# A gated MLP with LoRA, then a LoRA output layer, on one core: three small reorderings of who does what when

## The reference, cut to what matters

```python
x = x.reshape(8, 256, 1024)                       # f32, 2048 tokens of 1024 features
# layer 0: gate, up and down, each with a LoRA pair chosen by batch (rank 16)
gate = x @ W_gate.T + 0.5 * (x @ A_gate[i0[b]].T) @ B_gate[i0[b]].T       # 2752 features
up   = x @ W_up.T   + 0.5 * (x @ A_up[i0[b]].T) @ B_up[i0[b]].T
act  = silu(gate) * up
x = x + act @ W_down.T + 0.5 * (act @ A_down[i0[b]].T) @ B_down[i0[b]].T
# layer 1: output layer with its own adapters
x = x + x @ weight.T + bias + scale[i1[b]] * (x @ a_out[i1[b]].T) @ b_out[i1[b]].T
```

## Time and profile before

| | us |
|---|---|
| median of three runs (1677.37 to 1678.23) | 1678.08 |
| the profiled execution's own time | 1679.92 |
| its span, first to last instruction | 1678.2 |
| PE busy | 1625.1 (97%) |
| DVE busy | 1130.0 (67%) |
| POOL busy | 661.6 (39%) |
| ACT busy | 501.7 (30%) |
| mean granted TensorE clock | 0.990 |

### The profile page before, as it was taken

The page is one execution under the profiler, slowest core; times in us unless marked ns, Lnnn a source line. Parts: engine busy times, 40 slices in busy tenths (PEclk is TensorE's granted clock), DMA queues, the critical chain, the costliest instruction groups (busy, mean ns, idle before and its releaser), DMA issues.

```text
span 1678.2 us, 20940 instructions
## 1 busy us (share of the span) xinstructions
PE 1625.1 (97%) x7060; PEld 1318.2 (79%) x7060; DVE 1130.0 (67%) x1298; ACT 501.7 (30%) x833; POOL 661.6 (39%) x445
## 2 busy tenths in 40 slices
PE   5799999999998999999999999999999999899998
PEld 4588888888876888888888778888888887678886
DVE  4977777777768777777776655666665577766343
ACT  3543333333345433333334221111111122331100
POOL 4255444444452544454444443333332331541110
PEclk9899999999999999999999999999999999999999
DMA  8344434423532334344334751122222220113322
GB/s 151 81 104 105 141 92 108 150 79 84 136 89 78 102 104 142 93 115 141 82 89 129 246 146 60 48 79 79 79 57 73 69 63 13 26 31 78 79 46 56
DMA packets 218126, 156.13 MB, mean 93 GB/s; under 512 B 110692, under 2 KB 200164, under 8 KB 215268
## 3 DMA queue, kind: packets, MB, share of 16 engines
q1 hardware_dynamic: 170048, 115.18, 27.2%
q10 hardware_dynamic: 47844, 39.59, 7.4%
q0 software_dynamic: 128, 0.00, 0.0%
HBM read 115.38 MB, written 39.32 MB: 92 GB/s over the span
## 4 chain that ended last, share of the span: by engine, by line
PE 65%; DVE 1%; DMA 1%; SPq 1%; issue 0%; ACT 0%; DVEq 0%
PE ps L1892 65%; DMA Ad_raw<-in_L_cond_A_down_dram 1%; SPq L1261 0%; DVE acc L915 0%; SPq L1243 0%; DVE turned L850 0%; DVE Bd L861 0%; DVE Ad_turned L874 0%; DVE xt L593 0%; DVE ct L1033 0%; DVE turned L845 0%; DVE Td L933 0%; DVE c21buf L675 0%; DVE co L1055 0%; ACT W L1349 0%
## 5 line engine op out<-in xcount | busy, mean ns | idle before, releaser
L1892 PE MATMUL ps<-act,Wd 128*128 128x512 f32 x2016 | 463.7, 390 | 2.7 <-DVE acc L915 1.6
L1892 PE MATMUL ps<-X_T,W 128*128 128x512 f32 x1944 | 461.9, 393 | 0.4 <-DVE X_T L597 0.3
L1892 PEld LDWEIGHTS ps<-act,Wd 128*128 128x128 f32 x2016 | 379.2, 188 | 84.0 <-DVE acc L915 2.5
L1892 PE MATMUL ps<-X_B,W 128*128 128x512 f32 x1728 | 420.1, 393 | 20.1 <-DVE X_B L597 17.4
L1892 PEld LDWEIGHTS ps<-X_T,W 128*128 128x128 f32 x1944 | 366.0, 189 | 83.9 <-DVE vbuf L662 5.2
L1892 PEld LDWEIGHTS ps<-X_B,W 128*128 128x128 f32 x1728 | 326.9, 189 | 91.9 <-issue 19.8
L915 DVE TENSOR_TENSOR acc<-acc,ps 128x1024 f32<-128x1024 f32 x176 | 214.3, 1220 | 186.1 <-PE ps L1892 185.7
L1778 POOL TENSOR_TENSOR W<-s,W 128x512 fp32r<-128x512 f32 x156 | 211.5, 1357 | 233.6 <-ACT W L1349 233.6
L1778 POOL TENSOR_TENSOR W<-TG,W 128x512 fp32r<-128x512 f32 x88 | 129.9, 1477 | 158.1 <-ACT W L1349 158.0
L1349 ACT ACTIVATE W<-s 128x512 fp32r<-128x512 f32 x156 | 98.6, 632 | 278.1 <-PE ps L1892 278.1
L1818 POOL TENSOR_TENSOR act<-stage,act 128x1024 fp32r<-128x1024 f32 x42 | 100.6, 2413 | 175.3 <-ACT act L1568 175.3
(11 more groups left out here) (134 smaller groups left out, 1525.9 us busy)
## 6 DMA issues: line engine op xcount, KB each, us to landing
stage<-act_scratch SPq DMA_DIRECT2D x21, 1024.0 KB, 5.0
raw<-in_L_cond_W_gate_dram SPq DMA_DIRECT2D x164, 128.0 KB, 3.0
raw<-in_L_cond_W_up_dram SPq DMA_DIRECT2D x164, 128.0 KB, 3.1
raw<-in_x_dram SPq DMA_DIRECT2D x104, 128.0 KB, 3.4
raw<-in_L_cond_W_down_dram SPq DMA_DIRECT2D x88, 128.0 KB, 3.2
act_scratch<-c21buf ACTq DMA_DIRECT2D x42, 256.0 KB, 2.4
act_scratch<-vbuf ACTq DMA_DIRECT2D x42, 256.0 KB, 2.8
xt_scratch<-xt ACTq DMA_DIRECT2D x4, 2048.0 KB, 7.4
```

What stands on the lines that cost most here:

```text
L1892: return nc.tensor.matmul(dst, stationary, moving, start=start, stop=stop, skip_group_check=True)
```

## The change

Four things are moved. (1) VectorE's `b_low(U + 1)` goes from the end of `first_unit` to just behind the `t_low` calls, in both halves. (2) VectorE turns `Bd` 2 and 3 in block 9 (the tenth), after its additions number 12 and 13, rather than in the last block; `bd_high(2)` and `bd_high(3)` go before and behind `x1_high(0, 0)` on ScalarE, and `bd_low(2)` and `bd_low(3)` behind the additions (1, 0) and (3, 0) of the last block. (3) At the start ScalarE issues the index tables ahead of the first gate tile, then waits for them, reads two indices and issues the gate half of the first LoRA A rows (8 DMAs); SyncE issues only the up half, and issues `load_x_pair(6)` ahead of it rather than behind all 16. (4) The first product of all does high by high for both of its tiles first, then low by high, then high by low, waiting for each kind of part apart; and VectorE turns the first up tile ahead of the two first `x_low`.

```diff
@@ VectorE
                 for p in range(2):
                     for w in range(2):
                         t_low(h, p, w)
+                b_low(U + 1)
                 x_low(h, "T2", 0)
...
                 x_sum(h, "T4", 1)
-                b_low(U + 1)
...
                     elif bb == BLOCKS - 3 and n in (12, 14):
                         turn_item(("Bd", (n - 12) // 2))
+                    elif bb == BLOCKS - 2 and n in (12, 13):
+                        turn_item(("Bd", n - 10))
...
                         td_low(1, 1)
-                        turn_item(("Bd", 2))
-                    elif (k, pr) == (6, 0):
-                        turn_item(("Bd", 3))
-                        bd_low(2)
-                    elif (k, pr) == (7, 0):
-                        bd_low(3)
+                    elif (k, pr) in ((1, 0), (3, 0)):
+                        bd_low(2 + k // 2)
...
             turn_x(("x", 0, 1))
+            turn_tile(("U", 0))
             x_low(0, "B11", 0)
             x_low(0, "B21", 0)
-            turn_tile(("U", 0))
@@ SyncE
-                for w, a_all in enumerate((a_gate[0], a_up[0])):
...
+                for w in (range(1, 2) if item == ("Ag", 0, 0) else range(2)):
+                    ag_rows(sp, buf, filled, w, [l0[h * 4 + 2 * p + b] for b in range(2)])
...
                         load_x_pair(4)
+                        load_x_pair(6)
...
                     load_ag(item)
-                    if item == ("Ag", 0, 0):
-                        load_x_pair(6)
@@ ScalarE
-            load_first(eng, "G", w_gate)
             for n, table in enumerate((l0_index, l1_index)):
                 eng.dma_start(indices[...], ...).then_inc(indices_loaded, 16)
+            load_first(eng, "G", w_gate)
+
+            eng.wait_ge(indices_loaded, 2 * 16)
+            first_rows = [eng.value_load(indices[:, b:b + 1], ...) for b in range(2)]
+            n = raw_at["Ag", 0, 0]
+            ag_rows(eng, raw[n % RAW], raw_full[n % RAW], 0, first_rows)
...
-            for k in range(5):
+            bd_high(2)
+            x1_high(0, 0)
+            bd_high(3)
+            for k in range(1, 5):
                 x1_high(0, k)
             td_high(1)
-            x1_high(0, 5)
-            bd_high(2)
-            x1_high(0, 6)
-            bd_high(3)
-            x1_high(0, 7)
+            for k in range(5, KT):
+                x1_high(0, k)
@@ TensorE
+            def very_first(dst):
+
+                for wl, xl in ((0, 0), (1, 0), (0, 1)):
+                    for e in range(2):
+                        item, region = f"A1{e + 1}", f"B{e + 1}1"
+                        if (wl, xl) == (0, 0):
+                            eng.wait_ge(w_hi, w_at[0, item] + 1)
+                            eng.wait_ge(x_hi.sem, x_hi.after((0, region, 0)))
+                        elif (wl, xl) == (1, 0):
+                            wait_w_low(eng, 0, item)
+                        else:
+                            wait_x_low(eng, 0, region, 0)
+                        for j in range(2):
+                            matmul(dst, ring[w_at[0, item] % RING][:, wl, j, :], XR[region][:, xl, j, :],
+                                   start=(wl, xl, e, j) == (0, 0, 0, 0))
...
-                plain_part(U, "a", a, 1, 1, 0)
+                if U == 0:
+                    very_first(a)
+                else:
+                    plain_part(U, "a", a, 1, 1, 0)
```

More of the change, by code:

```diff
@@ L447, in load_first, with ag_rows @@
                               rows[:, 0:2 * NQ:2, c * HQ:(c + 1) * HQ]).then_inc(first_full[kind], 16)
+        def ag_rows(eng, buf, filled, w, rows_of):
+            for b, row in enumerate(rows_of):
+                rows = (a_gate[0], a_up[0])[w][bass.ds(row, 1), :, :].rearrange("o r m -> (o r) m")
+                for q in range(NQ):
+                    eng.dma_start(buf[q * Q + b * R:q * Q + (b + 1) * R, w * HQ:(w + 1) * HQ],
+                                  rows[:, q * HQ:(q + 1) * HQ]).then_inc(filled, 16)
         def store_out(eng, m, c, qs=range(NQ)):
@@ L1177, in load_ag @@
                 buf, filled = slot(item)
-                for w, a_all in enumerate((a_gate[0], a_up[0])):
-                    for b in range(2):
-                        rows = a_all[bass.ds(l0[h * 4 + 2 * p + b], 1), :, :].rearrange("o r m -> (o r) m")
-                        for q in range(NQ):
-                            sp.dma_start(buf[q * Q + b * R:q * Q + (b + 1) * R, w * HQ:(w + 1) * HQ],
-                                         rows[:, q * HQ:(q + 1) * HQ]).then_inc(filled, 16)
+                for w in (range(1, 2) if item == ("Ag", 0, 0) else range(2)):
+                    ag_rows(sp, buf, filled, w, [l0[h * 4 + 2 * p + b] for b in range(2)])
             def load_b(item):
@@ L1329, in _ @@
                               ).then_inc(indices_loaded, 16)
+            load_first(eng, "G", w_gate)
+            eng.wait_ge(indices_loaded, 2 * 16)
+            first_rows = [eng.value_load(indices[:, b:b + 1], min_val=0, max_val=a_gate.shape[1] - 1) for b in range(2)]
+            n = raw_at["Ag", 0, 0]
+            ag_rows(eng, raw[n % RAW], raw_full[n % RAW], 0, first_rows)
             made = [0]
```

## The result

| | before | after |
|---|---|---|
| median of four runs each, us | 1678.15 | 1666.19 |
| lowest and highest, us | 1677.37, 1678.24 | 1663.70, 1668.35 |
| profiled execution, us | 1679.92 | 1668.35 |
| its span, us | 1678.2 | 1666.6 |
| PE busy, us | 1625.1 | 1624.7 |

The ratio of the times is 0.9929, with an interval of 0.9912 to 0.9946: faster by 12.0 us, where 17.1 were forecast. By the profiled executions it is 11.6 us. That of after is the slowest of its four. Their spread is 4.65 us and that of before 0.87 (2.3 to 2.9 in the 9 to 15 executions of before that ran beside the experiments); what can be said of it comes with the experiments. One execution of the experiment e10 took 2333.14 us at a granted clock of 0.656 and is left out of all numbers.

The account below looks back on a forecast made before the run. TensorE was taken as the bound, busy 1625.1 of 1678.2 us, with VectorE's list limiting what its stalls give back. Gains of 8.4 + 8.1 + 0.6 = 17.1 us from 1678.08 gave 1661.0 us, range 1655.5 to 1667.0.

Parts of the forecast that it names:

- Term 1: `b_low` moved sooner in both halves: 4.2 us gained in each, 8.4 us together, the rest given back through VectorE's list.
- Term 2: `Bd` in the last block: wait of 5.6 us and 2.9 us of clock go, less 0.4; 8.1 us, bounds 7.3 and 8.8.
- Rival A: Both halves: VectorE's list doesn't bind and the stalls vanish whole; 19.4 us in place of 8.4, to 1650.0; chance 0.07.
- the 3.8 us go away once TensorE is early: Ahead of P4 in unit 2: VectorE's 3.8 us waiting for a ScalarE copy, itself waiting for TensorE, vanish.
- The rest of the list is work: Second half, last `t_low` to P4's addition: of 37.6 us, VectorE waits only 3.8 and 0.4 us.
- the overlaps with GpSimd that it feared: Unit 2: VectorE's two-input operations stretch while GpSimd works; one more overlap costs 1.1 us, two cost 2.2.
- starts 0.8 us later, by the dearer price of the second: Last block: at worst the t rows' chain starts 0.8 us later behind the two `bd_low`; 0.4 us was taken.
- a half clock in the last block in spite of the missing stall: Sign that the forecast is wrong; if right, the clock was to stay at 1.00 from 1440 on.
- Term 3: The start: second up tile comes about 0.6 us sooner; 0.6 us gained, bounds -2.4 and +1.5.
- rival C: The start costs: late A rows push the t rows and everything up to `b_low`; 2.4 us lost, 1664.0; chance 0.11.
- Rival B: Unit 2: waits move to the low parts of S1 to S3, each half keeps only 2 us; 1665.4; chance 0.15.
- Rival D: Slower: ScalarE's wait for the index tables delays the first matmul; 1682 or more; chance 0.02 with everything unforeseen.

Follow-up runs that it names:

- e10: Kernel before with only the `Bd` moves, plus GpSimd made to wait until all four t rows are masked; median 1670.10 us.
- e8: Changed kernel with one `x_low` (T2, behind `b_low`) computed twice, 1.2 us more in VectorE's list in each half; median 1668.28 us.
- e11: Changed kernel with four low parts of the second half (T1, T2) written for one of two k tiles, shortening VectorE's list; median 1664.54 us.
- e2: Kernel before with only the moves of `Bd` 2 and 3; median 1672.37 us.
- e5: Changed kernel with GpSimd holding its X1 low parts from the fourth on until all four t rows are masked; median 1661.75 us.
- e6: Changed kernel with SyncE issuing `load_x_pair(6)` behind its half of the A rows again; median 1663.77 us.
- e4: Kernel before with the `b_low` and `Bd` moves, without the start's parts; median 1666.67 us.
- e1: Kernel before with only `b_low` moved; median 1671.54 us.
- e3: Kernel before with only the start's parts, (3) and (4) of the change; median 1677.23 us.

## Why the prediction was right, and where it was too high

The time is 1666.19, within the range, 5.2 us above the forecast of 1661.0. The three gains come from where they were sought, and Terms 1 and 2 were each put over 2 us too high. Term 1 is one of size. In Term 2 a mechanism was missing: what GpSimd does to the chain of the t rows. The time stayed within the range since that was wide enough for it, not since the term's own bounds were.

**Term 1, 8.4 us (4.2 each half); measured 3.0 and 3.3.** The step that held is the main one: most of the 9.1 us can't be kept since VectorE's list binds. Rival A (nothing binds, 19.4 us) is refuted by e8 and e11: 1.2 us more in the list came out as 1.25 and 1.3 at P4, and 1.25 less as 1.2. The slack of 1.1 us in front of P4 was had in full. The step that failed is "the 3.8 us go away once TensorE is early": 0.8 of them stayed, since ScalarE makes that copy among its high parts of the sums, the first of which waits 4.20 us for VectorE's own sum (until 539.12). With 0.6 instead of 0.5 for `b_high`, and 0.6 us of waiting for the up tile that stay where 0.4 were to go, the count gives 3.3. Two of its errors hide each other in that. "The rest of the list is work" left out waits of 0.35 and 0.31 us (at 550.16 and 553.69 in the kernel before), which went too. And the overlaps with GpSimd that it feared changed places, at a price of about 0.7 us in sum: the first sum of unit 2 takes 1.75, where it took 0.68, the one that took 1.78 now 0.69, and another pair just ahead of P4 swaps in the same way (1.48 and 0.69, now 0.69 and 1.61). The bounds, 2.6 and 4.8, hold the result.

**Term 2, 8.1 us; measured 5.8 in the profiled executions, 6.3 by the median of e2.** This is the term that was mis-sized most, and outside its bounds. The Bd wait and its half clock were worth 8.4 behind their place (5.6 + 2.9 = 8.5 forecast). But the t chain ahead of it was put at 0.4 us and costs 1.8 us of stall and 1.3 to 2.5 of clock. (The table shows 1.2 and 1.4, since in the profiled execution of before TensorE came to its stall 0.6 us later than in all others, counted from matmul 4001.) The step that failed is the one that priced the chain by its start alone ("starts 0.8 us later, by the dearer price of the second"): it did start about 0.5 later, but two masks ahead of TensorE's restart then stood longer against GpSimd. I had named the mechanism in Term 1, even with its price, and not applied it to the chain. e5 and e10 show it: with GpSimd held, the last stretch gives 9.6 us in place of 5.8 (704.7 to 695.0), more than the 8.1 of the forecast, as the stall that stood there before shrinks too. What I had written as the sign of an error, a half clock in the last block in spite of the missing stall, is what came.

The Trainium skill (SBUF — State Buffer, Who interferes with whom) says that a VectorE instruction with two SBUF inputs contends with a GpSimd instruction that reads SBUF, and that one with at most one SBUF input, outside the two-port performance modes, doesn't. The trace agrees with both halves: while GpSimd was busy, the masks took 2.60 and 1.32 us, and the additions with one PSUM input next to them 0.68. Applied to each instruction of the chain in the forecast, that rule would have picked out the two masks.

**Term 3, 0.6 us; measured 0.5 by the ends of `t_low`, between 0 and 1.4 by the medians.** The size was right, the working was not, so that is luck. The A rows were to come 1.2 us later and came 2.9 later (2.1 to 2.9 in the six executions): SyncE issued the last at 28.13 rather than 27.3, and from there to the transpose it took 2.1 us, where 1.3 had been assumed. The second up tile, on which the gain rests, came 0.7 us sooner in the mean all the same, where 0.6 had been said. What the late A rows cost stood only in the term's lower bound and in rival C: e6, which takes it back, ends the last `t_low` over 3 us sooner and the whole 2.4. So rival C had the mechanism, though not the sign: the start didn't lose against before.

Rival B (given back, 2 us each half) was wrong in size, as each half kept 3.0 to 3.3, though TensorE does wait for GpSimd's low parts in unit 2, as it said (1.8 us). Rival D didn't occur: ScalarE waited for the index tables without harm, and the first matmul came 1.8 us sooner.

What stays open: whether the clock near 490 us is why e4 gives 1.4 less than e1 and e2 in sum, and why it fell in some executions and not in others. The wait of 3.48 us ahead of the first half's unit 2 the profile gives only as "issue"; it ends at 80.55, 0.2 us behind GpSimd's low part of W from TG (78.08 to 80.34), as that of 1.00 us in the second half ends at 537.86, 0.2 behind the same instruction there (535.38 to 537.65). So that part is the likely releaser; the wait stands ahead of P4 and doesn't move it.

## What to carry to other kernels

When an instruction of a long list is moved up, count the list from there to the next point at which TensorE needs it; what the stall gives is what that list has in idle time, here 3 us of 9. When work is shifted in time, go through each VectorE instruction in front of TensorE's next wait and ask whether both its inputs are in SBUF and what GpSimd does at that moment; one added wait, which kept GpSimd idle for 3.2 us until a chain on VectorE was through, was worth 4 us here. And look at which loads a product hangs on: here eight small ones issued ahead of 1 MB of tokens, rather than behind it, were worth 2.4 us, while the tokens still came sooner than in the kernel before.

## What the runs showed of the hardware that I had not expected

- The price of a short stall isn't fixed. Behind one and the same wait of 3.1 us at one and the same instruction, the granted clock over the next 8.00 us was 0.62 in two profiled executions and 0.79 in five; behind 0.6 us it was 1.00 each time. Behind the 5.6 us stall of `Bd` it was 0.65 over 8.37 us in the kernel before, 0.68 in e1 and 0.81 in e3, which have the same instructions there. Even a wait of 1.9 us, which TensorE has near 485 us in before, after and e1, was followed by half clock in the first two (0.94 from 480 to 510 us) and not in the third (1.00).
- What a VectorE instruction with two SBUF inputs loses to GpSimd is what is left of GpSimd's instruction, whatever its own size. All masks and `Td` low parts that met a 128x1024 subtraction ended 0.54 to 0.55 us behind its end, in before, after, e2 and e5. And it can lose more than once in a row: two `Td` low parts that take 1.28 us together took 4.52 in e5, each held for one subtraction.
- Issuing 256 KB DMAs took far longer while many were under way: 15.63 us for twelve in the changed kernel, with 212 GB/s moving from 17 to 22 us, against 2.01 for four in e6, issued from 22.49 on behind the small loads. That time is the issuing engine's, and all loads behind it wait as well.
